# Attention with layer norm on one core: dense products between the score pairs, reciprocals inside a job duo, aggregates gathered, and the last output finished by VectorE

## The reference

```python
xn = layernorm(x)                                   # over the 256 channels
q = relu(xn @ Wq.T + bq); k = relu(keys @ Wk.T + bk); v = relu(values @ Wv.T + bv)
# 16 heads of 16 channels; keys and values have one batch, shared by all
score = einsum('bhsd,bhtd->bhst', qh, kh) / sqrt(16)
a = einsum('bhst,bhtd->bhsd', softmax(score), vh)
a = transpose(a, (0, 1, 3, 2)).reshape(q.shape)     # heads' channels ahead of positions
y = clip((xn @ sign(W).T) * scale + bias, -100, 100)
out = x + (a + xn) + y
```

## Time and profile before

| | us |
|---|---|
| timed runs, median of 3 | 2841.65 (2841.63 to 2842.5) |
| the profiled execution, its time | 2842.26 |
| the profiled execution, its span | 2840.4 |
| TensorE matmul busy | 2766.6 |
| ScalarE busy | 2449.8 |
| VectorE busy | 2337.9 |
| POOL busy | 938.4 |

### The profile page before, as it was taken

How to read it: one execution, slowest core, us unless ns; L and a number is a source line. 1 busy time by engine, 2 the same in 40 slices (tenths; PEclk the granted TensorE clock), 3 DMA queues, 4 the chain that set the end, 5 groups by cost and what they waited for, 6 DMA issues and landing times.

```text
span 2840.4 us, 61159 instructions
## 1 busy us (share of the span) xinstructions
PE 2766.6 (97%) x17860; PEld 1147.5 (40%) x17860; DVE 2337.9 (82%) x4578; ACT 2449.8 (86%) x2949; POOL 938.4 (33%) x845
## 2 busy tenths in 40 slices
PE   8899999999999999999999999999999999999996
PEld 4434344443434434444443444334444443444331
DVE  6788888888888888888888888888888888888940
ACT  4788988888888888888898888888888888888996
POOL 4304334241343314334242343314333242343001
PEclk8699999999999999999999999999999999999998
DMA  7111221121221121121121221121121121221111
GB/s 143 60 40 57 66 68 46 50 66 57 63 70 52 40 70 55 65 70 33 59 70 55 65 66 51 44 70 55 65 66 34 62 69 55 65 64 36 48 55 38
DMA packets 78636, 167.74 MB, mean 59 GB/s; under 512 B 28547, under 2 KB 32646, under 8 KB 76326
## 3 DMA queue, kind: packets, MB, share of 16 engines
q1 hardware_dynamic: 78374, 164.19, 19.2%
HBM read 36.71 MB, written 17.83 MB: 19 GB/s over the span
## 4 chain that ended last, share of the span: by engine, by line
PE 75%; issue 10%; DVE 5%; ACT 2%; POOL 1%; DVEq 0%; POOLq 0%; ACTq 0%
PE value_ps L611 29%; PE ring L633 27%; PE score_ps L597 13%; DVE mx L962 4%; ACT probs L809 2%; PE score_ps L677 1%; PE score_ps L662 1%; PE score_ps L679 1%; PE score_ps L666 1%; PE score_ps L664 1%; POOL fin L1100 1%; DVE excess L937 0%; PE ring L642 0%; DVE mx L937 0%; DVE sums L994 0%
## 5 line engine op out<-in xcount | busy, mean ns | idle before, releaser
L809 ACT ACTIVATE probs<-score_ps 128x1024 f32<-128x1024 f32 x2048 | 1992.4, 1024 | 228.4 <-PE score_ps L597 222.0
L962 DVE TENSOR_REDUCE mx<-ring 128x1 f32<-128x512 f32 x2952 | 1900.5, 684 | 239.6 <-PE ring L633 214.7
L633 PE MATMUL ring<-kstack,qstack 48*128 48x512 f32 x3444 | 1169.2, 468 | 16.1 <-DVE mx L962 3.7
L611 PE MATMUL value_ps<-probs,vones 128*32 128x512 f32 x8192 | 1091.6, 605 | 1.3 <-ACT taken L816 0.5
L633 PEld LDWEIGHTS ring<-kstack,qstack 48*128 48x128 f32 x3444 | 489.8, 183 | 1073.4 <-DVE mx L962 1037.9
L597 PE MATMUL score_ps<-qstack,kstack 51*128 51x512 f32 x4096 | 813.8, 415 | 9.6 <-ACT probs L809 4.7
L937 DVE CUSTOM_DVE_ANT_0 excess<-ring,excess 128x512 f32<-128x512 f32 x512 | 353.1, 690 | 137.4 <-PE ring L633 120.3
L1100 POOL TENSOR_TENSOR dense<-dense,affine 128x512 f32<-128x512 f32 x128 | 164.3, 1284 | 860.1 <-ACT dense L859 858.6
L597 PEld LDWEIGHTS score_ps<-qstack,kstack 51*128 51x128 f32 x4096 | 394.2, 186 | 122.7 <-ACT probs L809 61.3
L825 ACT ACTIVATE excess<-ring 128x512 f32<-128x512 f32 x492 | 293.6, 597 | 1.2 <-PE ring L633 0.9
L611 PEld LDWEIGHTS value_ps<-probs,vones 128*32 128x32 f32 x8192 | 161.4, 108 | 321.4 <-issue 289.5
(11 more groups left out here) (93 smaller groups left out, 1413.4 us busy)
## 6 DMA issues: line engine op xcount, KB each, us to landing
qstack<-parts SPq DMA_DIRECT2D x768, 64.0 KB, 2.5
fin<-taken SPq DMA_DIRECT2D x256, 128.0 KB, 2.9
xin<-x SPq DMA_DIRECT2D x16, 1024.0 KB, 5.2
base_cur<-base_new SPq DMA_DIRECT2D x16, 1024.0 KB, 5.5
fin<-recip SPq DMA_DIRECT2D x32, 512.0 KB
out<-fin SPq DMA_DIRECT2D x32, 512.0 KB, 2.6
qstack<-proj SPq DMA_DIRECT2D x256, 12.0 KB
kstack<-base_cur SPq DMA_DIRECT2D x16, 128.0 KB, 6.0
```

Source lines behind the costliest of these rows:

```text
L611: mm = pe.matmul(value_ps[h4 * 32:(h4 + 1) * 32, :], vones[:, 2 * tp + c, hh * HALF + side * PAIRS + 2 * g + j, :, :], probs[:, q % 2 * GR ...
L633: pe.matmul(ps[:, :], qstack[nh][rows, pair, st * P:(st + 1) * P], keys, start=True, stop=True).then_inc(s_mm, 1)
L809: nc.scalar.activation(probs[:, q % 2 * GROUP + u % GROUP, :], score_ps[src][:, :], ACT.Exp, scale=EXP_SCALE).then_inc(s_probs, 1)
L962: nc.vector.tensor_reduce(most, src[:, :], AX.X, ALU.max).then_inc(s_mx, 1)
```

## The change

- The four dense jobs move from "behind" in duos 2, 4, 6, 8 to "between" in duos 1, 3, 5, 7. The place "behind" is gone for jobs. The projections stay in duos 11 and 13.
- The reciprocal of the sums moves from the end of duo 7 to behind the "between" maximum: of duo 7 in the first half-step, of duo 9 in the second.
- The eight aggregates stand in one row ahead of the joining maximum (number 6 of the octet) of duo 23; the wait for the statistics stands ahead of number 5.
- The last half-batch's output is not packed, sent through DRAM and finished by POOL. VectorE takes reciprocals of the whole tile of sums, multiplies and adds, in two halves of 512 columns (`finish_end`), each as soon as its gathers have landed; SP writes each half out. All other outputs are finished as before.

```diff
-        JOB_DUOS = [[2, 4, 6, 8, 11, 13], [1, 3, 7, 9]]
+        JOB_DUOS = [[1, 3, 5, 7, 11, 13], [1, 3, 7, 9]]
-        RECIP_UNIT = 14
+        RECIP_DUOS = (7, 9)
         AGGREGATE_DUO = 23
+        JOINS = 6
...
-                for what in ("first", "between", "second", "behind"):
-                    if {"between": job and job[0] != "dense", "behind": job and job[0] == "dense"}.get(what, True):
+                for what in ("first", "between", "second"):
+                    if what != "between" or job:
...
+                if last and not (now or att):
+                    result = out[NB - 1].rearrange("(f p j) c -> f p (j c)", f=2, p=P)[1]
+                    for a in range(NA):
+                        cols = slice(a * BANK, (a + 1) * BANK)
+                        sp.wait_ge(s_end, 3 * a + 3)
+                        sp.dma_start(result[:, cols], fin[:, 1, cols]).then_inc(s_out, 16)
+                    return
...
-                    if "behind" in at:
-                        do_job(b, hh, *job, at["behind"])
...
-                    if "behind" in at:
-                        take_job(b, hh, *job, at["behind"])
...
+            def finish_end(a):
+                cols = slice(a * BANK, (a + 1) * BANK)
+                dve.wait_ge(s_gather[a], NB * 4 * 32)
+                nc.vector.reciprocal(fin[:, 1, cols], fin[:, 1, cols]).then_inc(s_end, 1)
+                dve.wait_ge(s_end, 3 * a + 1)
+                nc.vector.tensor_tensor(fin[:, 0, cols], fin[:, 0, cols], fin[:, 1, cols], ALU.mult).then_inc(s_end, 1)
+                dve.wait_ge(s_bcopy, NB * 16)
+                dve.wait_ge(s_end, 3 * a + 2)
+                nc.vector.tensor_tensor(fin[:, 1, cols].rearrange("p (q j) -> p q j", j=J),
+                                        base_cur[:, 1, cols].rearrange("p (q j) -> p q j", j=J),
+                                        fin[:, 0, cols].rearrange("p (j q) -> p q j", j=J), ALU.add).then_inc(s_end, 1)
...
+            def maximum(b, hh, n, d, at, prep):
+                if prep and d in STATS_DUOS and n % 8 in STATS_AHEAD:
+                    statistics(b, *ROW_TILES[2 * STATS_DUOS.index(d) + STATS_AHEAD.index(n % 8)])
+                if prep and d == AGGREGATE_DUO and n % 8 == JOINS - 1:
+                    dve.wait_ge(s_stats, (b + 2) * 8)
+                if prep and d == AGGREGATE_DUO and n % 8 == JOINS:
+                    for a, j in ROW_TILES:
+                        aggregate(a, j)
+                reduce_bank(b, hh, n, at)
...
             def half_step(b, hh, now, att, last, prep, ahead):
                 for d, at in enumerate(plan(hh, False, ROWS_DUO)):
-                    if prep and d == AGGREGATE_DUO:
-                        dve.wait_ge(s_stats, (b + 2) * 8)
+                    between, before, behind = maxima_of(d)
                     if now:
-                        for n in itertools.chain(*maxima_of(d)):
...
-                    if last and d == RECIP_UNIT // 2:
+                        for n in between:
+                            maximum(b, hh, n, d, at, prep)
+                    if last and (now or att) and d == RECIP_DUOS[hh]:
                         reciprocals(*last)
-                    if prep and AGGREGATE_DUO <= d < AGGREGATE_DUO + 4:
-                        for a, j in ROW_TILES[2 * (d - AGGREGATE_DUO):2 * (d - AGGREGATE_DUO) + 2]:
-                            aggregate(a, j)
+                    if now:
+                        for n in itertools.chain(before, behind):
+                            maximum(b, hh, n, d, at, prep)
             run(dve, half_step)
+            for a in range(NA):
+                finish_end(a)
...
-                if last:
+                if last and (now or att):
                     finish(*last)
```

More of the change, by code:

```diff
@@ L223, in attention_block @@
         s_out = sem("s_out")
+        s_end = sem("s_end")
         def wait(eng, s, value):
@@ L521, in half_step @@
                     gather(*last, 3)
+                if last and not (now or att):
[5 more added lines that the diff above has]
+                    return
+                if last:
                     pack_sums(*last)
-                if last:
                     spread_reciprocals(*last)
@@ L556, in _ @@
             run(sp, half_step)
-            sp.wait_ge(s_out, NB * 2 * 16)
+            sp.wait_ge(s_out, (NB * 2 - 1 + NA) * 16)
         @block.tensor
@@ L1074, in _ @@
                         aggregate(a, i)
+            def maximum(b, hh, n, d, at, prep):
[7 more added lines that the diff above has]
+                reduce_bank(b, hh, n, at)
+                if n >= TILES and not is_difference(n) and reductions(n - TILES) <= 5:
+                    split_maxima(b, hh, reductions(n - TILES) - 1, b * 2 * REDS + made(hh, TILES - 1))
```

## The result

The changed kernel takes 2816.11 us (median of 4 runs, 2815.86 to 2817.83) against 2841.82 us for the kernel before, timed beside it (4 runs, 2841.63 to 2842.5): a ratio of 0.9911, 95% interval 0.9899 to 0.9924. That is 25.7 us; 2816 was forecast.

The account below looks back on a forecast made before the run. TensorE (busy 97%) led the chain, but costs were priced by gaps between duos' weigh matmuls. Gains of 7.4 + 5.8 + 0.7 + 12.0 = 25.9 us gave 2816 us, range 2812 to 2823.5.

Parts of the forecast that it names:

- The clock of gaps: Whole kernel: time between the weigh matmuls of successive duos; plain gaps 2.80 us into odd, 2.13 us into even duos.
- Dense jobs: Dense products moved between the score pairs: gap 3.80 us instead of 3.93, gain 7.4 us over 60 jobs.
- the tile, by a hair: Duos with a moved dense job: the score tile freed by the first exponential ends last, about level with the job's streaming.
- Reciprocals: Second half-step's reciprocal moved from duo 7 to duo 9: gap 4.19 us instead of 4.60, gain 5.8 us in all.
- the cover: First half-step: a dense job beside the reciprocal hides it; without it 0.41 us returns per reciprocal, 12 us over 29.
- the row at 1507.98: Second half-step, duo 9: VectorE waits 1.57 us for the projection ahead of this row, so the 0.54 us reciprocal fits.
- Aggregates: Eight aggregates ahead of the joining maximum: gain 0.7 us, between a 2.8 us gain and a 1.5 us loss.
- The end: Tail behind the last gather, 19.5 us, becomes 7.5 us with VectorE finishing in halves: gain 12.0 us, between 10.4 and 12.3.
- (a): Rival, dense duos: evacuation holds up the second exponential, gap stays 3.93 us, nothing gained; 2823.4 us, chance 0.08.
- (b): Rival, VectorE late where its work is gathered: aggregates lie bare, reciprocal keeps 0.2 us; 2826 us, chance 0.03.
- (d): Rival: the loop doesn't change, supposed causes being consequences, and only the tail gains 12 us; 2830 us, chance 0.03.
- (c): Rival: dense evacuation waits for POOL to free its buffer, holding up the second exponential; slower, 2847 us, chance 0.03.

## Why the prediction was right, and where it was not

**The clock of gaps.** It was the step that carried everything: each part was priced by a gap of the same trace, and the loop's 14.5 us (forecast 13.9) came out of such differences. The pattern has one exception that the prediction passed over, the gap where the loop is entered (2.97 us in the kernel before); the change left it as it was. That the sum is off by 0.2 us only is luck in part: the aggregates gave 1.0 us more than forecast and the end 0.7 to 0.8 less, and the two cancel.

**Dense jobs.** 3.80 us forecast from the turn, 3.80 measured. The reason given (the tile, by a hair) is shown by two kernels: half the products leave 3.80, a quarter more give 3.98, and the margin is 0.06 us. In the last batch 0.1 us was forecast and nothing came (3.86 against 3.87): the gap there is as long behind weigh as between the pairs.

**Reciprocals.** 5.7 us forecast and 0.41 x 14 = 5.7 measured. What failed is the cover: "if that cover were gone, 0.41 us would be back" names the job as what hides the instruction, and in duo 9 of the first half-step, without a job, it costs nothing at the same place. The idle time I read ahead of the row at 1507.98 was there and is used (1.02 us in place of 1.57), but duo 9 of the first half-step shows that a place can do without it. It isn't so everywhere: in duo 7 without a job, behind a duo that ends in a dense job, the same place costs 0.09 us. The other half of the statement, that the first half-step's reciprocal is free only beside a dense job, holds for the old place: with the dense job moved away and the reciprocal left, it costs 0.23 us.

**Aggregates.** 0.7 us forecast, 0.12 x 14 = 1.7 measured; the gap was forecast at 2.94 and is 2.87. The same error, it seems: the slack ahead of the join is more than the idle time shown. Twice the number costs the whole second row, so the slack is used up.

**The end.** 12.0 us forecast, 11.2 to 11.3 measured. The reciprocal is right to the hundredth (3.35), so the fixed share of 0.15 us and 6.2 ns a column carry over from 64 to 512 columns. The Trainium skill ("VectorE: DVE Perf Modes", First, the fixed hardware budget) states a repeat count of 8 for the reciprocal; the 4.3 us that the prediction worked out from it as an estimate are not borne out by the 3.35 us measured. The page gives no time for a column; that the count means eight cycles for each was the prediction's reading. What the prediction cites from the Trainium skill, "DMA: Bandwidth & Descriptors", Anatomy of one DMA, is stated there for DMAs on the gpsimd path, and all DMAs here are SP's; the sum didn't use it. Two terms were too small in the profiled execution: the sum, 1.04 us where 0.72 was taken and 0.85 was the bound, shown by the straight sum of 0.69; and the last output of 256 KB, 2816.0 - 2812.99 = 3.0 us where 2.6 were taken. The first is shown. The second is not: over the eleven kernels with the halved output it takes 2.50 to 3.51 us, 2.76 in the median, and one of 512 KB took 3.0 us in both kernels that have it, so half the bytes may well save a quarter of a microsecond, and one execution can't tell.

**The rivals.** (a) is excluded by the gap of 3.80, (b) by 4.18 and 2.87, (d) by the old end, which gives back 11.2 us and not 25.7. (c) never came near: among the changed kernel's waits a dense evacuation waits for POOL once, 3.3 us in the start-up, and the kernel before has that one too (3.6 us). A rival that I had not listed was nearer than (c): the loop's end. The change leaves TensorE's number of instructions as it was (17860 matmuls in both), and the gap into duo 0 stayed at 2.13 us in the loop. Why sixteen matmuls fewer in the body cost 1.3 us a passage, and eight more nothing, stays open: the traces show that the shorter jobs leave no delay behind them, so the program itself is what is left, not by which rule. The listed chances have a slip: without (c) they add up to 0.97, where the text has 0.96.

## What to carry to other kernels

Price a moved piece of work by the same slot elsewhere in the same trace: find a job that already stands where the new one will, and read what ends last there, not how long the job is. Idle time shown ahead of one instruction is a lower bound of the slack, since a row of merged instructions hides small waits; where an instruction stands in the order of buffers matters more than how much idle time surrounds it. Edits that share a resource should be undone singly, as the sum of the single losses (8.6 + 10.2 + 0.5 + 11.2 = 30.5 us here) is more than the gain when one leans on another.

## What the runs showed of the hardware

- A reciprocal of VectorE takes 0.544 us for 64 columns and 3.35 us for 512, with straight operands or with both reordered alike. A sum of 512 fp32 columns takes 0.69 us straight and 1.04 to 1.08 us with one operand read at a stride of 128 columns, in pieces of four.
- Removing 16 matmuls from a loop body of TensorE made 12 of 13 passages over a microsecond longer at the loop's end (15.6 us in all); adding 8 did nothing there and took 0.86 us off the entry of the loop.
- Matmuls with a weight load of 128x128 each started 0.12 us apart with 256 columns and 0.11 us apart with 128.
- The granted TensorE clock came back from its lower level at about 121 us in one execution and 125 us in another, after the same idle stretch ahead of it, worth 1.4 us of the time.
- The last output DMA took 2.50 to 3.51 us to the end of the span with 256 KB (eleven executions) and 3.0 us with 512 KB (two executions).
